# A graph network's matrix build: one bit a unit in place of five loaded counts a pair of units

## The reference

```python
x = _layernorm(x + _L0_gnn_ref(x, src, dst, L0_gnn_W, L0_gnn_b))             # 3 propagations over the edge counts
x = _layernorm(x + _L1_gnn_ref(x, edge_index, edge_attr_64, ...))            # an MLP on every edge
x = _layernorm(x + _L2_gnn_ref(x, src, dst, edge_weight, L2_gnn_gamma))      # 2 propagations with edge weights
x = _layernorm(x + _L3_gnn_ref(x, edge_index, L3_gnn_W, ...))                # 1 propagation over the edge counts
# a propagation is jax.ops.segment_sum(value[src], dst)
# setup_inputs: dst = int(6250 * uniform ** 2), sorted; src = randint(0, 6250)
```

## Time and profile before

| | |
|---|---|
| median of 3 runs | 6122.54 us (6121.46 to 6124.3) |
| the profiled execution's own time | 6138.58 us |
| its span | 6136.7 us |
| matrix build, first unit to last | 167.4 to 1992.5 us of the span |
| mean granted TensorE clock over the span | 0.796 of full speed |

### The profile page before, as it was taken

How to read it: one execution, slowest core, us unless ns; L and a number is a source line. 1 busy time by engine, 2 the same in 40 slices (tenths; PEclk the granted TensorE clock), 3 DMA queues, 4 the chain that set the end, 5 groups by cost and what they waited for, 6 DMA issues and landing times.

```text
span 6136.7 us, 124499 instructions
## 1 busy us (share of the span) xinstructions
PE 4264.3 (69%) x39029; PEld 3305.5 (54%) x39030; DVE 2691.1 (44%) x4704; ACT 1041.6 (17%) x2054; POOL 1961.2 (32%) x2919
## 2 busy tenths in 40 slices
PE   1788888877667789892666666666666677477394
PEld 0566666666556789892444444444444433233194
DVE  8777777766555220214444444444444300300414
ACT  1012223345656000001111111111111000100100
POOL 3333332221000000002777777777777300000000
PEclk6999999988888899996555555556555699799697
DMA  2012233346676889866333333333333399599394
GB/s 83 9 39 84 80 106 108 109 152 191 203 225 207 302 340 389 332 243 118 78 78 81 77 78 80 78 77 78 80 77 78 111 418 418 213 418 418 130 358 175
DMA packets 443167, 1061.51 MB, mean 173 GB/s; under 512 B 127013, under 2 KB 285543, under 8 KB 414216
## 3 DMA queue, kind: packets, MB, share of 16 engines
q1 hardware_dynamic: 390985, 1003.20, 46.3%
q0 software_dynamic: 52096, 57.38, 4.9%
HBM read 815.58 MB, written 244.81 MB: 173 GB/s over the span
## 4 chain that ended last, share of the span: by engine, by line
PE 22%; POOL 20%; DVE 19%; issue 15%; DMA 12%; DVEq 7%; ACT 2%; SPq 1%; ACTq 1%; POOLq 1%
POOL WORK L686 20%; PE banks L1606 13%; DMA T<-dense_w 9%; DVE X L914 5%; DVE T L914 4%; PE banks L1640 3%; PE banks L1691 3%; DVEq L391 2%; DMA WORK<-table,idx 2%; DVEq L914 1%; PE banks L1632 1%; ACTq L391 1%; DVE X L921 1%; DVE T L921 1%; DVEq L921 1%
## 5 line engine op out<-in xcount | busy, mean ns | idle before, releaser
L686 POOL DMA_INDIRECT WORK<-table,idx x1568 | 1487.6, 949 | 1321.3 <-DVE idx L1038 843.6
L1606 PE MATMUL banks<-WORK,T 125*128 125x192 bf16 (+1 forms) x10000 | 834.7, 247 | 61.5 <-DVE WORK L1082 61.5
L1606 PEld LDWEIGHTS banks<-WORK,T 125*128 125x128 bf16 (+1 forms) x10000 | 832.2, 99 | 64.0 <-issue 47.3
L1563 PE MATMUL banks<-T,WORK 128*128 x1568 | 274.9, 293 | 766.6 <-DVE WORK L994 766.6
L1691 PE MATMUL banks<-T,WORK 125*64 125x391 f32 (+1 forms) x3200 | 573.8, 499 | 230.5 <-DMA T<-dense_w 189.0
L1563 PEld LDWEIGHTS banks<-T,WORK 128*128 128x128 bf16 x1568 | 218.8, 140 | 797.6 <-issue 797.6
L646 POOL TENSOR_TENSOR T<-T 128x6 f32 x1182 | 359.8, 327 | 870.2 <-DVE X L921 741.1
L1640 PE MATMUL banks<-X 128*128 128x125 bf16 x7092 | 549.1, 226 | 68.8 <-DVE X L921 63.4
L1640 PE MATMUL banks<-T 128*128 128x125 bf16 (+1 forms) x7500 | 578.1, 239 | 0.2 <-DVE T L921 0.2
L1016 DVE TENSOR_TENSOR WORK<-banks,WORK 128x512 f32<-128x512 f32 x196 | 135.6, 692 | 1002.3 <-DMA WORK<-table,idx 997.9
L1640 PEld LDWEIGHTS banks<-X 128*128 128x128 bf16 x7092 | 461.0, 116 | 210.5 <-DVE X L921 200.5
(11 more groups left out here) (364 smaller groups left out, 4420.1 us busy)
## 6 DMA issues: line engine op xcount, KB each, us to landing
T<-dense_c SPq DMA_DIRECT2D x200, 1562.5 KB, 8.4
T<-dense_w SPq DMA_DIRECT2D x200, 782.0 KB, 10.3
T<-dense_w SPq DMA_DIRECT2D x200, 780.5 KB, 10.4
dense_w<-WORK SPq DMA_DIRECT2D x125, 1093.8 KB
WORK<-rel_rows SPq DMA_DIRECT2D x197, 256.0 KB, 3.8
WORK<-in_eaT SPq DMA_DIRECT2D x392, 128.0 KB
dense_c<-T SPq DMA_DIRECT2D x13, 3125.0 KB, 14.8
dense_c<-ACC SPq DMA_DIRECT2D x12, 3125.0 KB, 15.1
```

What stands on the lines that cost most here:

```text
L686: nc.gpsimd.indirect_dma_start(out=g_sb[:, u, c * D:(c + 1) * D], out_offset=None, in_=table, in_offset=bass.IndirectOffsetOnAxis(ap=idx[: ...
L1563: T.matmul(z, lhsT, QW12[:, ds(at * 2, P)], start=c in (0, 2), stop=False, skip_group_check=True)
L1606: last = T.matmul(banks[0:cols, 2 * u + s, 0:3 * D], a_rows[:, u, h * WAYS + s * LO:h * WAYS + s * LO + cols], x123[:, h, :], start=h == 0 ...
```

## The change

The running sums are no longer stored. VectorE prepares, at the end of the set-up and on partition 0, one word a unit (the steps of its first block in the low 12 bits, of its second in the high ones: `words_sb`, 314 words) and 13 words of 24 bits, one bit a unit that says whether it has any extra step (`spells_sb`).

In the build VectorE and TensorE run 13 outer turns of 12 inner turns of 2 units, and the last unit by itself. A turn of the outer loop loads one word of bits. After a unit's first part each of the two engines tests its bit: where it is set, it loads the unit's word (one value), unpacks it, adds it to a running register, and runs the loops of steps as before; where it is clear, it does nothing more. GpSimd goes on as before, by its own table.

ScalarE loads nothing. TensorE closes each block with a matmul of one column of zeros (`close`) that adds nothing and raises `block_done`, for which alone ScalarE waits. In a unit with a set bit each block's close stands behind its steps; both stand behind the first parts of both blocks of the unit. In a unit with a clear bit both closes follow the whole unit.

```diff
+WORD = 12
+SPELL = 24
+SPELLS = UNITS // SPELL
...
-        offs_sb = X_full[0:1, 5600:5600 + P * BATCH].bitcast(I32)
+        steps_sb = X_full[0:1, 5600:5600 + P * BATCH].bitcast(I32)
+        words_sb = X_full[0:1, 3200:3200 + UNITS + 1].bitcast(I32)
+        spells_sb = X_full[0:1, 6240:6240 + SPELLS].bitcast(I32)
+        marks, carried, spelt = (ACC_full[0:1, i * UNITS:i * UNITS + SPELLS * SPELL] for i in range(3))
...
-        def offs_of(eng, block, n):
-            return loads(eng, offs_sb[0:1, ds(block, n)], 0, BLOCKS * COLS)
+        def bounded(eng, value):
+            return nc.s_assert_within(eng.snap(value & MASK), 0, BLOCKS * COLS, skip_runtime_bounds_check_because="steps are counted up to the last one")
+        def offs_of(eng, steps, high, u):
+            word = eng.value_load(words_sb[0:1, ds(u, 1)], min_val=0, max_val=COLS << WORD | COLS)
+            offs = [bounded(eng, eng.snap(steps))]
+            offs.append(bounded(eng, offs[0] + (word & (1 << WORD) - 1)))
+            eng.reg_alu(high, word, WORD, ALU.logical_shift_right)
+            offs.append(bounded(eng, offs[1] + eng.snap(high)))
+            eng.reg_mov(steps, offs[2])
+            return offs
+        def spell_of(eng, spell, w):
+            eng.reg_mov(spell, eng.value_load(spells_sb[0:1, ds(w, 1)], min_val=0, max_val=(1 << SPELL) - 1))
+            return nc.s_assert_within(eng.snap(w * (SPELL // 2)), 0, UNITS // 2 - SPELL // 2, skip_runtime_bounds_check_because="there are so many spells")
...
@@ VectorE, set-up @@
+                V.tensor_copy(steps_int, block_more)
...
+                dve.wait_ge(tables_loaded, 32)
+                fin(V.tensor_scalar(words_sb, steps_sb[:, 1:2 * (UNITS + 1):2], WORD, None, ALU.logical_shift_left))
+                at("high steps")
+                fin(V.tensor_tensor(words_sb, words_sb, steps_sb[:, 0:2 * (UNITS + 1):2], ALU.bitwise_or))
+                at("words")
+                V.tensor_scalar(marks, words_sb[:, 0:SPELLS * SPELL], 0, None, ALU.is_gt)
+                fin(V.memset(carried, 2.0))
+                at("carried")
+                fin(V.memset(carried[:, SPELL - 1::SPELL], 0.0))
+                at("marks")
+                fin(V.tensor_tensor_scan(spelt[:, ::-1], carried[:, ::-1], marks[:, ::-1], 0.0, ALU.mult, ALU.add))
+                at("spelt")
+                fin(V.tensor_copy(spells_sb, spelt[:, 0::SPELL]))
...
@@ VectorE, build_dense @@
-                with dve.Fori(0, UNITS // 2) as i:
-                    offs = offs_of(dve, i * 4, 5)
-                    for v in range(2):
-                        unit(i * 2 + v, v, offs[2 * v:2 * v + 3])
-                unit(UNITS - 1, 0, offs_of(dve, BLOCKS - 1, 2))
+                with dve.Fori(0, SPELLS) as w:
+                    from_unit = spell_of(dve, spell, w)
+                    with dve.Fori(from_unit, from_unit + SPELL // 2) as i:
+                        for v in range(2):
+                            first_one_hots(i * 2 + v, v)
+                            first_weights(i * 2 + v, v)
+                            dve.reg_alu(mark, spell, 1 << v, ALU.bitwise_and)
+                            with dve.If(dve.snap(mark) > 0):
+                                mores(offs_of(dve, steps, high, i * 2 + v))
+                        dve.reg_alu(spell, spell, 2, ALU.logical_shift_right)
...
@@ ScalarE, batch @@
-                past = offs_of(act, n * BATCH + 1, BATCH)
...
-                    act.wait_ge(first_used, n * BATCH + (b + 1 + 2 * SLOTS))
-                    act.wait_ge(more_used, past[b] + SLOTS)
+                    act.wait_ge(block_done, n * BATCH + (b + 1))
...
@@ TensorE, build_dense @@
-                    with pe.If(offs[blocks] > offs[0]):
-                        for h, (begin, past) in enumerate(zip(offs, offs[1:])):
...
+                def close(bank):
+                    T.matmul(banks[:, bank, 0:1], iota2[:, :, 0], none, start=False, stop=False, skip_group_check=True).then_inc(block_done, 1)
+                def mores(v, offs):
+                    for h, (begin, past) in enumerate(zip(offs, offs[1:])):
+                        with pe.If(past > begin):
+                            with pe.Fori(begin, past, 2) as s:
+                                more(s, 2 * h, UNIT * v + QUAD * h)
+                                with pe.If(past > s + 1):
+                                    more(s + 1, 2 * h + 1, UNIT * v + QUAD * h)
+                        close(UNIT * v + QUAD * h)
...
+                with pe.Fori(0, SPELLS) as w:
+                    from_unit = spell_of(pe, spell, w)
+                    with pe.Fori(from_unit, from_unit + SPELL // 2) as i:
+                        for v in range(2):
+                            unit(i * 2 + v, v, 2)
+                            pe.reg_alu(mark, spell, 1 << v, ALU.bitwise_and)
+                            with pe.If(pe.snap(mark) > 0):
+                                mores(v, offs_of(pe, steps, high, i * 2 + v))
+                            with pe.Else():
+                                for h in range(2):
+                                    close(UNIT * v + QUAD * h)
+                        pe.reg_alu(spell, spell, 2, ALU.logical_shift_right)
+                unit(UNITS - 1, 0, 1)
+                mores(0, offs_of(pe, steps, high, UNITS - 1)[0:2])
```

More of the change, by code:

```diff
@@ L222, in gnn_kernel @@
         table_int = T12[:, 11400:11400 + TABLE].bitcast(I32)
+        steps_int = T12[:, 11480:11480 + BATCH].bitcast(I32)
         lanes = T12[:, 12200:12200 + P]
@@ L339, in gnn_kernel @@
                                  "offset", "columns", "span", "count", "small", "kept", "start", "start_int", "large", "more", "block_more", "base", "row_tot",
-                                 "off0", *[f"off{c}" for c in range(1, BATCH + 1)], "delta", "offs_int", "table")
+                                 "off0", *[f"off{c}" for c in range(1, BATCH + 1)], "delta", "offs_int", "table", "high steps", "words", "carried", "marks", "spelt", "spells")
         at_flag = Steps().stage(1, "most", "all_most", "many", "thrice", "passes", "inexact_int", "passes_int", "rounds")
@@ L1653, in more, with unit @@
                     last.then_inc(more_used, 1)
-                def unit(u, v, offs):
-                    plane, blocks = first_planes[:, v, :], len(offs) - 1
+                def unit(u, v, blocks):
+                    plane = first_planes[:, v, :]
                     pe.wait_ge(first_hots, u + 1)
@@ L1675, in build_dense @@
-                with pe.Fori(0, UNITS // 2) as i:
-                    offs = offs_of(pe, i * 4, 5)
-                    for v in range(2):
-                        unit(i * 2 + v, v, offs[2 * v:2 * v + 3])
-                unit(UNITS - 1, 0, offs_of(pe, BLOCKS - 1, 2))
+                def close(bank):
[8 more added lines that the diff above has]
+                        close(UNIT * v + QUAD * h)
@@ new lines, in build_dense @@
+                steps, high = pe.alloc_register("steps"), pe.alloc_register("high")
+                pe.reg_mov(steps, 0)
+                spell, mark = pe.alloc_register("spell"), pe.alloc_register("mark")
+                pe.wait_ge(first_hots, 1)
+                with pe.Fori(0, SPELLS) as w:
[10 more added lines that the diff above has]
+                        pe.reg_alu(spell, spell, 2, ALU.logical_shift_right)
```

49 lines of the change are left out of this document (29 added, 20 removed).

## The result

| | before | changed | difference |
|---|---|---|---|
| median of 3 runs, us | 6122.54 | 6224.99 (6214.21 to 6231.37) | +102.5 |
| ratio, 95% interval | | 1.0165 (1.0141 to 1.0188) | slower by 1.65% |
| the profiled execution, its span | 6138.58, 6136.7 | 6224.99, 6223.2 | +86.5 in the span |

A later group of runs gave 1.0142 (1.0127 to 1.0158). The forecast was 6125, in a range up to 6190: wrong. The profiled execution of before was 16.0 us over its own median, that of the changed kernel was its median; so the two traces differ by 86.5 us where the medians differ by 102.5.

The account below looks back on a forecast made before the run. VectorE's own lines and sequencer bound the first stretch, VectorE's and ScalarE's slow loads weigh in the last. Set-up +3.5, first stretch +101, middle -11 and tail -90 give +3.5 us: 6125 us, range 6060 to 6190.

Parts of the forecast that it names:

- the price of a marked unit: Units with extra steps, to 1387 us: 1.2 us each, 167 us; under 0.8 or over 1.5 would prove the prediction wrong.
- the tail: Build from 1499 to 1992 us, 140 units nearly all without extra steps: 2.88 us a unit, -90 us.
- the stop at the counts store: Last stretch: ScalarE waits 5 us for a free batch buffer once in five batches, when a store of counts comes between.
- the late close: Last stretch: ScalarE waits for the whole unit; 2.45 us a unit, hidden under 2.88, otherwise up to 0.3 us a unit.
- Set-up: End of the set-up on VectorE: seven dependent operations on one partition, all seen, +3.5 us (2 to 6).
- Marked units, the load: VectorE, between products and steps: one-value load of 0.31 us plus half the delay from stores, 0.50 us with its gap.
- a load costs what it costs, one value or five: Rival, between products and steps: 1.7 us a marked unit, +78 us, 6201 us; chance 0.18.
- Marked units, the unpacking: VectorE, between products and steps: some eight operations for three masks, net five at 0.075 us, 0.38 us.
- 139 times: Units 0 to 143: the price of 1.2 us is paid in each of 139 units with extra steps, 167 us.
- TensorE follows VectorE: First stretch: TensorE's test, load, unpacking and closes fit in VectorE's added 1.2 us; if not, 29 us longer.
- The middle: Build from 1387 to 1499 us: loads removed -21, 12 marked units +14, unmarked units -4, together -11 us.
- The rival of the late close: Last stretch: TensorE's clock falls in the waits, 3.2 us a unit, -45 instead of -90, 6171 us; chance 0.06.

Follow-up runs that it names:

- The run without bounds on VectorE: Changed kernel with the assertion behind the one-word load removed on VectorE alone; median 6181.6 us, ratio 1.0072 to the kernel before.
- the run with three ready offsets: Changed kernel, but each set unit bit loads three ready offsets instead of one packed word, with nothing unpacked; median 6253.3 us, ratio 1.0204 to the kernel before.
- TensorE without bounds: Changed kernel with the assertion behind the one-word load removed on TensorE alone; median 6215.3 us, ratio 1.0124 to the kernel before.
- the runs with an early load: Changed kernel with test and load moved ahead of products (VectorE, 6216.3 us), or test, load and unpacking ahead of first matmuls (TensorE, 6303.3), or both (6290.4).
- the run with counts stored last: Changed kernel with 25 counts stores moved behind the build, output not the reference's; read by its last 139 units alone, 339.3 us against 434.7.
- the run with the early close: Changed kernel, but in clear-bit units TensorE closes the first block right behind its own matmuls, ahead of the second block's; median 6202.5 us, ratio 1.0115 to before.
- a third buffer: Three dense_w batch buffers instead of two: 6008.0 us on the kernel whose loop one count splits, 6132.7 us on the kernel before.

## Why the prediction was wrong

Its order of events was right in each stretch; two sizes were off, by 34 and 33 us to the same side. The first is the price of a marked unit, in which the unpacking was put too low and the assertion at nothing; the second is the tail, with the stop at the counts store too short and the late close at nothing.

- *Set-up*: +4.9 for +3.5, inside its bounds; it scatters from 170.4 to 172.3 between the two profiles of the changed kernel.
- *Marked units, the load*: 0.50 us was foreseen with its gap; the mean in units 12 to 143 is 0.51. Right, and so was its reason, that stores make the mean longer than the median (last section). The rival "a load costs what it costs, one value or five" fell: one value had a median of 0.31 in 139 loads. That rival's price of 1.7 us a unit nearly came, but from elsewhere. The Trainium skill's floor of about 600 ns for a register load ("DMA: Bandwidth & Descriptors", section "Latency and other measured facts") doesn't agree with these 0.31 us.
- *Marked units, the unpacking*: this is the step that failed. "Some eight operations where three masks stood, net five at 0.075, 0.38 us" is 0.74 us: the assertion that the load's bounds bring (0.30) was not counted at all, and the eight instructions take 0.68, where the three masks took 0.24 around (815.33 to 815.50 and 815.61 to 815.68). Test and address, put at 0.29, took 0.32. A marked unit costs 1.45 us more with a load of the median length and, as the mean load is 0.20 over the median, 1.65 us in all instead of 1.2, which is above the 1.5 that the prediction named as a sign of being wrong. The run without bounds on VectorE confirms the assertion's part, 37.9 us, and the run with three ready offsets the 0.75 of both together.
- *139 times*: it should have been 127. Units 0 to 11, with 14.6 steps each, took 275.7 and 275.3 us; the price is hidden once a unit of many steps waits for others. So the sum is 127 x 1.65 = 210, less 66 loads of five at 0.99 (0.55 by the medians, 0.44 by which the mean load is over its median) = 65: 145, and 7 more if the outer turns cost what was forecast, against 135.0 measured for units 12 to 143. The full-clock sizes, 1.39 and 0.79, make it 202 - 69 = 133, or 140 with the turns. So this part is known to some 10 us either way.
- *"TensorE follows VectorE"*: right for the changed kernel (TensorE without bounds: 1.3 us). No number of the prediction said how much room it has: the runs with an early load show too little of it in units of three steps and more, and that TensorE's pauses cost it clock.
- *The middle*: -1.2 for -11, the same price of a marked unit and longer loads (0.71 us in the mean there).
- *The tail*: the bound went to the store ring, as forecast, at 3.13 us a unit and not 2.88. The stop at a store of counts was put at 5 us in five batches; the run with counts stored last puts it at 8.6 against that run's 30.5, with the gain in clock in it, so that the 30.5 beside the forecast's 31 for the rest are in part luck. The late close, costed at nothing, is 12 of the 33 missing us, by the run with the early close: the ring of two batch buffers didn't cover it. The rival of the late close had this direction, but by a falling clock, and the tail's stayed at 0.89 (0.88 before). The DMA share rose to 0.77, not 0.83.
- *Sum*: +1.4 set-up, +34 first stretch, +10 middle, +33 tail turn +3.5 into +81.6. The other 21 of the 102.5 us are no part of the forecast: 5 lie behind the build, and 16 come from the profiled execution of before, which stood that far over its median.

## What to carry to other kernels

A load into a register is more than the load itself: count the assertion of its bounds, each mask and each branch as instructions of the sequencer, read the distance between the neighbours in time order, and ask which queued work of the engine they run under. Two engines that hand planes to one another gain from a cut on one only up to the other's lead: 0.3 us a unit came through everywhere here, 0.7 only in units of two steps or fewer. And before a slower stretch is put down to an engine's pauses, compare the same units at the same granted clock: here the pauses cost nothing at full clock, and all 76 us lay where TensorE had 1.2 GHz for a part of a unit in one run or the other. Where a flag is set almost everywhere in one part and almost nowhere in the rest, one count that splits the loop costs nothing in either part; here it turned +1.4% into -0.8%, and only then did a third buffer pay.

## What the runs showed of the hardware

- One load instruction took 0.31 us for one value, 0.59 for five and 0.76 for three (medians, VectorE, first stretch). Three and five come from the same table; the three start at an even entry of it, the five at every fourth. Whether the place or the number does it was not tried.
- Loads into registers were long only while the DMA engines were busy. Of VectorE's 127 one-value loads in units 12 to 143 of the changed kernel, 85 began with a DMA share of at most 0.1 in their first 0.3 us (the length of a short load): none took over 0.32 us, though 12 of them overlapped a load of another engine. The 40 that began with a share over 0.5 took 0.94 in the mean, up to 1.35. For five values (before) and three, each over the length of its short load, it is 37 loads, all but one under 0.60, against 22 with 1.80 in the mean, and 87 with none over 0.77, against 39 with 2.61. Loads that overlap one of TensorE's are the longest (five values: 27 with 1.69 in the mean, the others 0.59; three values: 36 with 2.67, the other 91 with 0.79), but nearly all of these fall in busy stretches, and a long load has more time to meet another. Whether a second load adds anything stays open.
- Register instructions behind 24 queued matmuls cost next to nothing on TensorE (its assertions: 1.3 us in 144 units). The same ones in an empty queue, with pauses of up to 2.71 us, cost nothing either in units that stayed at 2.4 GHz (21 units, 0.00 us in the median). But TensorE then had 86 pauses of over 2 us where there were 10, and 1.2 GHz for 314 us of units 12 to 143 where it was 113.
